# One attention stage of a two-FFN kernel: fewer and narrower TensorE products, denominators on GpSimd, fused steps in another order

## The reference

```python
# FFN (twice): x = x + 0.5 * ffn(layernorm(x)); T = 4096 rows of 256, E = 8, K = 2, capacity 640
xn = xf * rsqrt(mean(xf * xf) + eps)
topk_p, topk_i = top_k(softmax(xn @ router_w.T), K); rw = topk_p / sum(topk_p)
dispatch = first `capacity` rows of each expert
eout = (silu(xg @ rg) * (xg @ ru)) @ rd                 # I = 1024 per expert
routed = scatter_add(eout * weight)
shared = silu(x @ sg) * (x @ su) @ sd                   # I = 2048
# attention (once, between them): x = x + attn(layernorm(x)); 16 heads of 16, groups of 64 rows
q, k, v = split(xg @ w_qkv); q = rmsnorm(q, ln_w); k = rmsnorm(k, ln_w)
att = softmax(where(causal, q @ k.T / 4, -max))
return (att @ v) @ w_proj
```

## Time and profile before

| | |
|---|---|
| time, median of 3 runs | 2208.72 us (2208.45 to 2210.69) |
| the profiled execution | 2215.33 us, span 2213.3 us |
| busy: PE, PEld, DVE, ACT, POOL | 98%, 91%, 62%, 47%, 20% |
| mean granted clock of PE | 0.995 |
| fused stage | from about 670 to 1370 us of the span |

### The profile page before, as it was taken

How to read it: one execution, slowest core, us unless ns; L and a number is a source line. 1 busy time by engine, 2 the same in 40 slices (tenths; PEclk the granted TensorE clock), 3 DMA queues, 4 the chain that set the end, 5 groups by cost and what they waited for, 6 DMA issues and landing times.

```text
span 2213.3 us, 38807 instructions
## 1 busy us (share of the span) xinstructions
PE 2169.2 (98%) x14464; PEld 2005.1 (91%) x14464; DVE 1366.4 (62%) x3182; ACT 1037.1 (47%) x2004; POOL 437.3 (20%) x424
## 2 busy tenths in 40 slices
PE   7999999999999999999999999999999999999999
PEld 6888889999998899999998898888899999988887
DVE  6666546666665676777778786666466666533333
ACT  3233335555553666666666663333355555432222
POOL 2323211122112221122222232332112121200000
PEclk9999999999999999999999999999999999999999
DMA  9231224554445000000101101312244444441010
GB/s 271 94 106 56 72 60 128 133 149 100 101 105 153 20 3 18 20 20 1 34 1 49 44 11 56 118 64 72 61 101 105 109 101 101 106 133 58 29 58 20
DMA packets 194490, 168.42 MB, mean 76 GB/s; under 512 B 16905, under 2 KB 175037, under 8 KB 194304
## 3 DMA queue, kind: packets, MB, share of 16 engines
q1 hardware_dynamic: 176640, 144.57, 21.9%
q0 software_dynamic: 17664, 21.38, 5.6%
HBM read 104.32 MB, written 68.07 MB: 78 GB/s over the span
## 4 chain that ended last, share of the span: by engine, by line
PE 88%; DVE 7%; issue 2%; ACT 1%; DMA 1%; another core or an unknown queue 1%; SPq 0%; POOL 0%; DVEq 0%; ACTq 0%; POOLq 0%
PE gate_up_p L327 29%; PE quad L327 26%; PE out_p L365 20%; PE misc L365 4%; PE misc L495 3%; PE quad L512 3%; DVE h_s L967 1%; PE misc L391 1%; PE misc L383 1%; PE misc L402 1%; PE misc L400 0%; DVE y_s L1093 0%; DVE hl L971 0%; DMA stage<-in_L_ffn_rd 0%
## 5 line engine op out<-in xcount | busy, mean ns | idle before, releaser
L327 PE MATMUL gate_up_p<-zh,w 128*128 128x512 f32 (+2 forms) x2368 | 707.6, 362 | 2.4 <-DVE zl L839 2.3
L646 ACT CAST hh<-h_s 128x512 fp32r<-128x512 f32 (+2 forms) x512 | 277.4, 542 | 655.1 <-DVE h_s L967 621.3
L365 PE MATMUL out_p<-w,hh 128*128 128x256 f32 x2816 | 563.8, 282 | 6.0 <-DVE hl L971 5.3
L327 PE MATMUL quad<-zh,w 128*128 128x512 f32 (+2 forms) x1728 | 484.2, 348 | 0.0
L327 PEld LDWEIGHTS gate_up_p<-zh,w 128*128 128x128 f32 x2368 | 431.2, 189 | 54.5 <-DVE zl L839 2.8
L365 PEld LDWEIGHTS out_p<-w,hh 128*128 128x128 f32 x2816 | 458.6, 189 | 19.3 <-DVE hl L971 9.0
L327 PE MATMUL gate_up_p<-zl,w 128*128 128x512 f32 (+2 forms) x1184 | 423.7, 358 | 0.0
L365 PE MATMUL out_p<-w,hl 128*128 128x256 f32 x1408 | 394.1, 280 | 0.0
L327 PEld LDWEIGHTS quad<-zh,w 128*128 128x128 f32 x1728 | 309.9, 189 | 27.2
L971 DVE TENSOR_TENSOR hl<-h_s,hh 128x512 fp32r<-128x512 f32 (+2 forms) x432 | 247.8, 574 | 137.7 <-ACT hh L646 117.7
L967 DVE TENSOR_TENSOR h_s<-gate_up_p,sg_s 128x512 f32<-128x512 f32 (+2 forms) x296 | 178.2, 602 | 232.7 <-PE gate_up_p L327 218.3
(11 more groups left out here) (168 smaller groups left out, 2868.3 us busy)
## 6 DMA issues: line engine op xcount, KB each, us to landing
stage<-in_L_ffn_rg SPq DMA_DIRECT2D x128, 128.0 KB
stage<-in_L_ffn_ru SPq DMA_DIRECT2D x128, 128.0 KB
stage<-in_L_ffn_rd SPq DMA_DIRECT2D x128, 128.0 KB
slots_d<-empty SPq DMA_DIRECT2D x16, 662.5 KB, 7.8
zh_d<-zh SPq DMA_DIRECT2D x16, 512.0 KB
zl_d<-zl SPq DMA_DIRECT2D x16, 512.0 KB
y_d<-x SPq DMA_DIRECT2D x16, 512.0 KB
zh<-zh_d SPq DMA_DIRECT2D x16, 512.0 KB, 4.3
```

The lines of the kernel that those rows point to most:

```text
L327: last = pe.matmul(dst, a, b, start=(k == 0), stop=(k == 3 * n - 1))
L365: last = pe.matmul(out[:, j // 2, o:o + C], a[:, par, cols], w[:, hi, :], start=(c == 0 and i == 0 and j % 2 == 0), stop=(c == NCH - 1 and ...
L646: nc.scalar.copy(hh[:, n % 2, 0:ncol], h_s[:, n % 2, 0:ncol]).then_inc(sm["hh_done"], 1)
```

## The change

The values product has `vh` and `vl` side by side in one tile `vv`: one product of `ph` with both (128 columns) and one of `pl` with `vh` (64 columns) take the place of three. The ones columns are gone; GpSimd adds up the rows of p_s in a tree of seven adds, three after the exponential (`row_sums_half`) and four later in the step (`row_sums`). `outputs` on DVE adds the two halves of the product, then multiplies by the reciprocal. The transposes of qcat and kcat take 112 columns instead of 128. Half of the score products have 66 stationary columns. azn moves from DVE to GpSimd. On PE gate stands ahead of the transposes of qcat, y_s and azn; on DVE `extras(s - 1, 1)` stands behind `stats`, and `extras(s, 0)` behind `outputs`. Outside the fused stage the second half of expert block 0's row transposes stands ahead of `down`, and the load of z for s1 behind two weight pieces. `itok` shares memory with the start's buffers. Left out here are waits' counts, the allocations and the arguments' names.

```diff
     MAXSLOT = E * CAP - 1
...
 
@@ -154,8 +155,7 @@
         qcat = sb("qcat", [P, NH, 64], F32, att)
         kcat = sb("kcat", [P, NH, 64], F32, att)
...
                 if k is not None:
                     route_product(f, k)
-                if (b, c) in XR_AT:
+                if (b, c) in XR_AT and (b, c) != max(XR_AT):
                     row_transposes(f, 0, XR_AT[(b, c)])
 
             def blocks(f, phase, todo):
@@ -455,6 +457,8 @@
                         if c == 1:
                             out_free(f, phase, b)
                         prev = chunk_before(f, phase, b, c)
+                        if phase == "s0" and (b, c) == max(XR_AT):
+                            row_transposes(f, 0, XR_AT[(b, c)])
                         if prev:
                             down_of(*prev)
...
-            def pair_transposes(src, done):
+            def pair_transposes(src, rows, done):
                 for j in range(NH // 2):
-                    last = pe.transpose(misc[:, j // 4, (j % 4) * P:(j % 4 + 1) * P],
-                                        src[:, 2 * j:2 * j + 2, :].rearrange("p h d -> p (h d)"), ident[:, :])
+                    last = pe.transpose(misc[0:rows, j // 4, (j % 4) * P:(j % 4 + 1) * P],
+                                        src[:, 2 * j:2 * j + 2, :].rearrange("p h d -> p (h d)")[:, 0:rows], ident[:, :])
                 last.then_inc(sm[done], 1)
...
                     o = (j % 4) * P
-                    for g in range(2):
+                    for g, rows in ((1, P), (0, GROUP + 2)):
                         own = slice(GROUP * g, GROUP * g + GROUP)
-                        last = pe.matmul(quad[:, j // 4, o:o + P].rearrange("p (r c) -> p r c", r=2), q_t[:, j, g, :],
-                                         k_t[:, j, :, own], start=(g == 0), stop=(g == 1))
+                        last = pe.matmul(quad[0:rows, j // 4, o:o + P].rearrange("p (r c) -> p r c", r=2), q_t[:, j, g, 0:rows],
+                                         k_t[:, j, :, own], start=(g == 1), stop=True, skip_group_check=(g == 0))
...
                 for j in range(NH // 2):
-                    o = (j % 4) * 66
-                    last = split_product(quad[:, j // 4, o:o + 66], [(ph[:, j, :], pl[:, j, :], vh[:, q, j, :], vl[:, q, j, :])], 1)
+                    o = (j % 4) * P
+                    pe.matmul(quad[:, j // 4, o:o + P], ph[:, j, :], vv[:, q, j, :, :].rearrange("p a c -> p (a c)"), start=True, stop=False)
+                    last = pe.matmul(quad[:, j // 4, o:o + 64], pl[:, j, :], vv[:, q, j, 0, :], start=False, stop=True)
                 last.then_inc(sm["a_y"], 1)
...
+                if c == 0:
+                    ready(f, phase, b)
+                loaded(f, phase, b, c)
+                gate(n, b % 2, c, buf, SB)
                 if uses:
                     pe.wait_ge(sm["misc_free"], max(uses) + 1)
-                if c == 0:
-                    ready(f, phase, b)
                 if keys is not None:
                     pe.wait_ge(sm["a_qlo"], keys + 1)
                     wait(pe, sm["a_pl"], keys - 1)
-                    pair_transposes(qcat, "a_qt")
+                    pair_transposes(qcat, QKROWS, "a_qt")
                 if out is not None:
                     y_transpose(out)
                 if z is not None:
                     z_transpose(z)
-                loaded(f, phase, b, c)
-                gate(n, b % 2, c, buf, SB)
                 if out is not None:
                     project(out)
                 if keys is not None:
                     pe.wait_ge(sm["a_qe"], keys + 1)
-                    pair_transposes(kcat, "a_kt")
+                    pair_transposes(kcat, QKROWS, "a_kt")
...
-                last = nc.scalar.copy(q_t[:, :, g, own], pairs[:, :, own])
+                last = nc.scalar.copy(q_t[0:QKROWS, :, g, own], pairs[0:QKROWS, :, own])
...
+                v.memset(k_t[96:128, :, 1, :].bitcast(F32), 0.0).then_inc(sm["a_pad"], 1)
+                v.memset(q_t[96:128, :, 0, 0:GROUP].bitcast(F32), 0.0).then_inc(sm["a_pad"], 1)
+                v.memset(q_t[96:128, :, 1, GROUP:P].bitcast(F32), 0.0).then_inc(sm["a_pad"], 1)
...
-            def normal(t):
-                m = t % 2
-                dve.wait_ge(sm["a_rs"], t + 1)
-                wait(dve, sm["a_t"], t)
-                v.tensor_scalar(azn[:, :], xtile(t), amv[:, m, 0:1], ard[:, m:m + 1], ALU.subtract, ALU.mult).then_inc(sm["a_zn"], 1)
...
-                        last = v.tensor_tensor(vl[rows, q, :, o:o + HD], src, vh[rows, q, :, o:o + HD], ALU.subtract)
+                        last = v.tensor_tensor(vv[rows, q, :, 1, o:o + HD], src, vv[rows, q, :, 0, o:o + HD], ALU.subtract)
...
             def masked(t):
                 dve.wait_ge(sm["a_s"], t + 1)
                 wait(dve, sm["a_pt"], t)
+                wait(dve, sm["a_half"], t)
...
             def outputs(t):
                 dve.wait_ge(sm["a_y"], t + 1)
                 wait(dve, sm["a_yt"], t)
-                yp = quad[:, :, 0:4 * 66].rearrange("p b (j c) -> p b j c", c=66)
-                rd4 = rden[:, :].rearrange("p (b j r) -> p b j r", b=2, r=2)
-                for b in range(2):
-                    last = v.reciprocal(rd4[:, b, :, :], yp[:, b, :, 64:66])
-                last.then_inc(sm["a_rden"], 1)
-                dve.wait_ge(sm["a_rden"], t + 1)
+                yp = quad[:, :, :].rearrange("p b (j a c) -> p (b j) c a", a=2, c=64)
                 for g in range(2):
                     rows = slice(64 * g, 64 * g + 64)
-                    for b in range(2):
-                        src = yp[rows, b, :, 32 * g:32 * g + 32].rearrange("p j (r d) -> p j r d", d=HD)
-                        dst = y_s[rows, :].rearrange("p (b j r d) -> p b j r d", b=2, r=2, d=HD)[:, b]
-                        last = v.tensor_tensor(dst, src, rd4[rows, b].unsqueeze(3).broadcast_to([64, 4, 2, HD]), ALU.mult)
-                last.then_inc(sm["a_yn"], 1)
+                    last = v.tensor_reduce(y_s[rows, :].rearrange("p (j c) -> p j c", c=2 * HD), yp[rows, :, 32 * g:32 * g + 32, :], AX, ALU.add)
+                last.then_inc(sm["a_ysum"], 1)
+                dve.wait_ge(sm["a_den"], t + 1)
+                v.reciprocal(rden[:, :], den_a[:, :]).then_inc(sm["a_rden"], 1)
+                dve.wait_ge(sm["a_ysum"], t + 1)
+                dve.wait_ge(sm["a_rden"], t + 1)
+                y_heads = y_s[:, :].rearrange("p (h d) -> p h d", d=HD)
+                v.tensor_tensor(y_heads, y_heads, rden[:, :].unsqueeze(2).broadcast_to([P, NH, HD]), ALU.mult).then_inc(sm["a_yn"], 1)
...
@@ -1120,8 +1121,6 @@
                     v.tensor_copy(k_t[64:128, :, 1, :], pairs[64:128]).then_inc(sm["a_ke1"], 1)
                 if s == 0:
                     half_low(0, NEB - 1, NCH - 1)
-                else:
-                    extras(s - 1, 1)
...
@@ -1140,18 +1139,18 @@
                     add_shared(0 if prev[0] == "s1" else 1, *prev)
                 if ahead is not None:
                     stats(ahead)
+                if s:
+                    extras(s - 1, 1)
                 if keys is not None:
                     masked(keys)
                 fused_low(n)
                 h_product(n + 1, SB)
                 if keys is not None:
                     subtracted(keys)
-                if ahead is not None:
-                    normal(ahead)
                 fused_low(n + 1)
-                extras(s, 0)
                 if probs is not None:
                     outputs(probs)
+                extras(s, 0)
...
-                g.memset(vh[:, :, :, :].bitcast(F32), 0.0).then_inc(sm["a_const"], 1)
-                g.memset(vl[:, :, :, :].bitcast(F32), 0.0).then_inc(sm["a_const"], 1)
-                pool.wait_ge(sm["a_const"], 2)
-                for r in range(2):
-                    g.memset(vh[64 * r:64 * r + 64, :, :, 64 + r:65 + r].bitcast(F32), 1.0).then_inc(sm["a_const"], 1)
-                pool.wait_ge(sm["a_const"], 4)
+                g.memset(vv[:, :, :, :, :].bitcast(F32), 0.0).then_inc(sm["a_const"], 1)
+                pool.wait_ge(sm["a_const"], 1)
+
+            def row_sums_half(t):
+                pool.wait_ge(sm["a_exp"], t + 1)
+                g.tensor_tensor(psums[:, :, :], p_s[:, :, 0:HD], p_s[:, :, HD:2 * HD], ALU.add).then_inc(sm["a_tree"], 1)
+                pool.wait_ge(sm["a_tree"], 5 * t + 1)
+                g.tensor_tensor(psums[:, :, :], psums[:, :, :], p_s[:, :, 2 * HD:3 * HD], ALU.add).then_inc(sm["a_tree"], 1)
+                pool.wait_ge(sm["a_tree"], 5 * t + 2)
+                g.tensor_tensor(psums[:, :, :], psums[:, :, :], p_s[:, :, 3 * HD:GROUP], ALU.add).then_inc(sm["a_half"], 1)
+
+            def row_sums(t):
+                pool.wait_ge(sm["a_half"], t + 1)
+                for level, wide in ((3, HD // 2), (4, HD // 4), (5, HD // 8)):
+                    g.tensor_tensor(psums[:, :, 0:wide], psums[:, :, 0:wide], psums[:, :, wide:2 * wide],
```

(16 more changed lines are left out.)

21 lines of the change are left out of this document (11 added, 10 removed).

## The result

| | before | after |
|---|---|---|
| time, median of 5 runs each, same chip | 2210.69 us | 2251.75 us (2249.73 to 2259.42) |
| ratio | | 1.0191 [1.0172, 1.0211] |
| span of the profiled execution | 2213.3 us | 2257.2 us |
| mean granted clock of PE | 0.995 | 0.989 |

What follows compares the result with a forecast made beforehand. The loop through GpSimd and the exponential, 19.05 us, was to overtake PE as the bound. Plain steps +4, steps with the add +8, clock +16.5, routing -4, last steps +2, outside -7.5: +19, 2228 us, range 2175 to 2262.

Steps and rivals of the forecast that it cites:

- the term for the routing steps: Fused steps that route the second FFN's tokens: -10 us for fewer waits, +6 for late route4 and ln_rows, sum -4.
- The bound and the loop: Fused stage: q_t copy to q_t copy through PE, ACT, DVE, GpSimd and the exponential decides, 19.05 us a plain step.
- The 2.34 us behind it: From the end of DVE's subtraction to the next q_t copy: 2.34 us, added whole to GpSimd's +16.7 for the loop.
- PE's terms: PE's work in a fused step: values -0.89 us, scores -0.43, transposes -0.22, leaving 17.3 us.
- The clock: PE's granted clock halves behind waits in half of 30 fused steps: +21 us, less 4.5 for earlier falls, +16.5.
- The second rival: Fused stage: the loop decides but PE's clock does not fall anew: 2207 us, chance 0.25.
- the tail: The last two fused steps, which have an output and little cover: +2 us.
- Outside: Outside the fused stage: load_z behind two weight pieces -6.8 us, earlier row transposes -0.7, together -7.5.
- GpSimd stays hidden: Fused stage: adds and their waits cost under 1.6 us, so PE decides: 2181 us, chance 0.30.
- The clock holds: Fused stage: the loop binds without new half-clock falls, 21 us less than forecast: 2207 us, chance 0.25.
- The dear adds: GpSimd's adds cost more: loop 20.2 us, clock falls in 25 steps, 2272 us, chance 0.10.
- DVE's new work: DVE's outputs, about 2.0 us against 1.3: y_s ready at about +17.7, PE asks at 19, so no cost.

## Why the prediction was right or wrong

The forecast was 2228 us, 19 more than before; the change cost 41. The step of the forecast that failed is the term for the routing steps, -4; the rest holds, in part by luck.

**The bound and the loop: right.** The changed kernel is bound by the loop from q_t copy through GpSimd and the exponential, as forecast: 19.17 us in plain steps (19.05 forecast) and 20.43 with the add (20.3). PE's wait ahead of the projection is 1.3 us.

**But two of its terms were wrong and cancelled.** azn was set at 0.45 us from DVE's 0.40 and took 1.23, plus 0.18 ahead of it; the later adds took 2.27 us against 1.5 set, and kcat 0.45 more than alone. GpSimd's half ended at +18.17 instead of +16.7. In return the 2.34 us behind it, which the earlier trace rows show behind DVE's subtraction, held a table load of 1.28 us. It ran ahead of the end of GpSimd's half (load at 890.35, half ended at 892.93), so only 1.0 us follows. I had taken the 2.34 as one piece without asking which of the two releasers it stands behind.

**PE's terms.** Values went from 2.60 to 889.58-887.88 = 1.70 us: right to 0.01. Scores gave 0.40 against 0.43. The 112-column transposes gave nothing: eight of them take 893.31-892.42 = 0.89 us, before 0.87, against 0.22 for 16 set. That the load shrinks with its columns held for the scores and not for these.

**The clock: wrong in plain steps, by the whole +16.5.** The second rival's view of the clock came true there. The size of the term came out all the same, by luck: of the three falls of before in the fused stage, the two ahead of the routing steps are gone, and new ones came only in the routing steps and behind them, where the forecast had them in half of all steps. By the means of the clock they cost some 20 us, before 5 in the whole fused stage: +15. Busy us by stretch of the changed kernel, plain steps and then the rest:

```profile
872.00:1110.00 238.00, 218.92 (x1531) 194.56 (x1529) 176.62 (x320) 149.63 (x282) 117.18 (x162) 1.00 0.05 18
1110.00:1330.00 220.00, 186.67 (x1232) 163.73 (x1233) 164.43 (x337) 125.32 (x230) 100.50 (x131) 0.94 0.08 26
```

With PE idle 19 of 238 us in waits of 1.3 us the clock stayed at 1.00. The Trainium skill (TensorE: Matmul & The Clock Gate, "Why this matters for your kernels") warns only of longer gaps; the plain steps agree with it. Yet with azn on DVE, where PE waited 0.91 us for y_s and 0.70 for yl in one step, the clock fell six times in the steps i = 2 to 19. In the kernel before it fell at 850.1 and at 1003.8, in steps for which the trace shows no wait of PE. A wait's length alone does not tell; what does stays open.

**The routing steps: the term that failed, -4 against +34.** I had bounded route4 behind stats at 12 us and credited -10 for the waits for y_s. Of the 34 us some 13 are the clock and some 5 the longer loop of these 11 steps, which the forecast has in other terms. By this estimate some 16 us remain where it had -4: 20 us of a miss of 22. The sum had the scatters and ln_rows, each priced by itself. It lacked what stands behind the moved step on every engine, in most of the routing steps. On DVE `extras(s - 1, 1)` came ahead of `masked` and of y_s. On GpSimd the inverse root for the second FFN, and in the step shown first the four scatters, came ahead of ard and the new denominators; there outputs waited for the denominators, zl waited behind outputs, and PE 6.30 us for zl. That single edit taken back, extras(s - 1, 1) in its old place, gave 27 to 32 us; the scatters' step is 4.8 of them. The rest of the 41 us is the plain and add steps and the tail (6.6, set at 2; some 5 of it the clock), less what the edits outside bring.

**Outside: right.** As an edit of its own it brought -8 us, -7.5 forecast. In the changed kernel's profiled execution it was -4.3. The first q_t copy came anywhere from 711.5 to 721.4 us in kernels with the same edits outside, so single executions can't price it better.

**The rivals.** GpSimd stays hidden: no, its half ended at +18.17, past the +16.1 it named. The clock holds: yes in plain steps, but its 2207 lacked the routing steps. The dear adds: their loop of 20.2 did not come, 19.17 did (and its sum sets 30 us for 25 falls, which are 35 at the forecast's 1.4 each). DVE's new work was set at nothing on y_s: true only while GpSimd decides. As soon as GpSimd's work was gone, y_s came last, at 19.0.

**What stays open**: azn alone on GpSimd cost 6 us, the mechanism not singled out; how the 27 to 32 us of the moved step divide among its parts; and why the clock falls behind short waits in some steps.

## What to carry to other kernels

A step that is moved must be followed on every engine that waits for it: here one moved call on an engine 62% busy cost some 30 us, spread over the routing steps. The mask and y_s stood in line behind it on its own engine, and an inverse root or four scatters, with a new sum behind them, waited for it on a second one. The third engine waited for the late operands, and in some steps then ran at half the clock for a while. An engine that is idle 80% of the time isn't free if its idle time lies outside the loop; add the new work to its row between its releaser and its last consumer, with durations of that engine, not of its neighbour. And saving work on the busiest engine is worth only the distance to the next loop: with 0.9 us saved, the loops through the exponential and through y_s decided, and the kernel that shortened these (outputs ahead of the last hl, the early table load), with the narrow operands, the edits outside and the old values product, took 2187 us.

## What the runs showed of the hardware

- ACT's table load (1.28 us) ran ahead of the wait for the last releaser in one case and behind it in the other. The code waits for GpSimd's half and then for DVE's. In the kernel before the load stood 0.08 us behind the end of DVE's half (869.51, half ended at 869.43). In the changed kernel it stood as close behind that (890.35, 890.27), but also behind ACT's own hh (890.32), so what released it there isn't told apart; that it did not wait for GpSimd's half, which ended at 892.93, is shown.
- A subtraction and product with two scalars per partition on 256 elements took 1.23 us on GpSimd and 0.40 on DVE; a two-input one of the same size took 0.73 on GpSimd.
- The product of y_s took 0.42 us alone and 0.85 beside GpSimd's adds, kcat 0.73 and 1.18, hl 0.68 and 1.53. The Trainium skill (SBUF — State Buffer, "SBUF: two separate sides") says that of a GpSimd operation and a DVE operation with two inputs in SBUF, the one that comes second waits for the other in full; the 1.53 agrees (0.99 us to the end of GpSimd's, and 0.54).
- 66 stationary columns made score products faster (16 in 1.41 us instead of 1.81), 112 in place of 128 made no difference in transposes.
